# GNN layer with residual norm on one core: in the drain, GpSimd makes the selectors, the floor of the messages moves to PSUM, and TensorE turns the selectors between the two halves of the message sums

## What is computed

```python
def _L0_gnn_ref(x, edge_index, edge_attr, W, b, gamma, beta):
    row, col = (edge_index[0], edge_index[1])
    msg_in = jnp.concatenate([x[row], x[col], edge_attr], axis=-1)
    h = msg_in @ W + b
    mu = jnp.mean(h, axis=-1, keepdims=True)
    var = jnp.mean(jnp.square(h - mu), axis=-1, keepdims=True)
    h = (h - mu) * jax.lax.rsqrt(var + LN_EPS) * gamma + beta
    msg = jax.nn.relu(h)
    return jax.ops.segment_sum(msg, row, num_segments=x.shape[0])

x = _layernorm(x + _L0_gnn_ref(x, jnp.stack([src, dst]), edge_attr_128, W, b, gamma, beta), axis=-1)
```

## Time and profile before

| | before |
|---|---|
| median of 3 runs (lowest to highest) | 1763.23 us (1761.63 to 1763.72) |
| the profiled execution's own time | 1767.91 us |
| its span, first to last instruction | 1766.0 us |
| mean granted TensorE clock over the span | 0.813 |
| TensorE (PE) busy | 1214.0 us, 69% |
| DVE busy | 960.2 us, 54% |
| ScalarE (ACT) busy | 718.9 us, 41% |
| GpSimd (POOL) busy | 770.3 us, 44% |

### The profile page before, as it was taken

How to read it: one execution, slowest core, us unless ns; L and a number is a source line. 1 busy time by engine, 2 the same in 40 slices (tenths; PEclk the granted TensorE clock), 3 DMA queues, 4 the chain that set the end, 5 groups by cost and what they waited for, 6 DMA issues and landing times.

```text
span 1766.0 us, 36601 instructions
## 1 busy us (share of the span) xinstructions
PE 1214.0 (69%) x10009; PEld 1061.0 (60%) x10010; DVE 960.2 (54%) x2822; ACT 718.9 (41%) x2854; POOL 770.3 (44%) x808
## 2 busy tenths in 40 slices
PE   6688766676676766666666666766666766647775
PEld 5555656666566665666666566665656666546662
DVE  7633345555455555445545545554455545439997
ACT  4223333434334443334434434443334433336766
POOL 0334555444454445455444455444555444550003
PEclk9778788778778878788887888787788778869998
DMA  7544444444434444444444444444344434313322
GB/s 213 165 116 130 134 145 146 128 113 120 138 116 129 129 117 116 123 130 130 123 115 122 130 122 129 127 112 131 112 130 128 127 111 119 108 57 91 90 67 73
DMA packets 184266, 214.69 MB, mean 122 GB/s; under 512 B 51478, under 2 KB 133610, under 8 KB 184080
## 3 DMA queue, kind: packets, MB, share of 16 engines
q1 hardware_dynamic: 158044, 159.86, 33.8%
q0 software_dynamic: 25088, 51.83, 8.4%
q10 hardware_dynamic: 948, 0.79, 0.2%
HBM read 145.91 MB, written 66.47 MB: 120 GB/s over the span
## 4 chain that ended last, share of the span: by engine, by line
PE 41%; another core or an unknown queue 22%; issue 18%; ACT 9%; DVE 6%; DMA 2%; DVEq 2%; SPq 0%; ACTq 0%
PE bank L956 11%; PE bank L934 7%; PE bank L910 7%; PE bank L850 5%; ACT late L1177 4%; PE bank L924 3%; PE bank L963 2%; DVE late L1573 2%; ACT turn L1139 2%; PE bank L840 1%; PE bank L838 1%; DVEq L490 1%; DMA tabB<-room 1%; ACT late L1183 1%
## 5 line engine op out<-in xcount | busy, mean ns | idle before, releaser
L677 POOL DMA_INDIRECT rows<-p,pos_idx x784 | 754.3, 962 | 825.4 <-ACT p L1143 537.3
L1139 ACT COPY turn<-bank 128x512 f32<-128x512 f32 x196 | 114.8, 586 | 705.1 <-remote 533.1
L956 PE MATMUL bank<-wc,turn 128*128 128x128 f32 x1552 | 300.8, 354 | 67.4 <-ACT turn L1139 54.7
L934 PE MATMUL bank<-room 128*128 x2640 | 251.8, 250 | 93.7 <-issue 67.2
L956 PEld LDWEIGHTS bank<-wc,turn 128*128 128x128 f32 x1552 | 260.5, 254 | 92.2 <-ACT turn L1139 77.5
L934 PEld LDWEIGHTS bank<-room 128*128 128x128 bf16 x2640 | 208.7, 115 | 115.1 <-issue 104.0
L1177 ACT ACTIVATE late<-room 128x128 f32<-128x128 f32 x880 | 260.7, 302 | 3.0 <-issue 1.5
L1573 DVE SCALAR_TENSOR_TENSOR late<-room,late,floor 128x128 f32<-128x128 f32 x880 | 252.6, 349 | 0.8 <-issue 0.5
L910 PE MATMUL bank<-late 128*128 128x129 f32 x1504 | 233.3, 299 | 25.9 <-issue 23.5
L910 PEld LDWEIGHTS bank<-late 128*128 128x128 f32 x1504 | 211.8, 215 | 18.6 <-issue 18.2
L1169 ACT COPY room<-bank 128x512 bf16<-128x512 bf16 x220 | 129.2, 587 | 210.6 <-remote 111.1
(11 more groups left out here) (237 smaller groups left out, 1255.4 us busy)
## 6 DMA issues: line engine op xcount, KB each, us to landing
p<-in_edge_attr_dram SPq DMA_DIRECT2D x98, 512.0 KB
room<-rows SPq DMA_DIRECT2D x264, 129.0 KB
near_bc<-near SPq DMA_DIRECT2D x98, 256.0 KB
late<-rows SPq DMA_DIRECT2D x176, 129.0 KB
rows<-p,pos_idx POOLq DMA_INDIRECT x784
rows<-fill SPq DMA_DIRECT2D x49, 129.0 KB, 3.2
win<-tabB SPq DMA_DIRECT2D x196, 31.5 KB
tabB<-room SPq DMA_DIRECT2D x12, 384.0 KB, 3.2
```

Source lines behind the costliest of these rows:

```text
L677: nc.gpsimd.indirect_dma_start(rows_ap, bass.IndirectOffsetOnAxis(pos_idx[:, k, j:j + 1], 0), stage[:, k, j, :], None).then_inc(st_free[k] ...
L934: mm = pe.matmul(bank[A_BANK + b2][:, jj * D:(jj + 1) * D], selT[b2][:, jj * P:(jj + 1) * P], tabA[:, bass.ds(at[jj // UJ], 1), part, :], ...
L956: pe.matmul(bank[H_BANK + h][:, t * D:(t + 1) * D], eT[h][:, t * P:(t + 1) * P], wc[:, 2, :], start=(t == 0), stop=False, skip_group_check ...
L1139: nc.scalar.copy(eT[h], bank[E_BANK][:]).then_inc(eT_ready, 1)
```

## The change

Four edits, all in the drain. From step `BY_POOL` = 178 on, GpSimd makes the selectors (those of pair 180 and later), as 4 `tensor_scalar` instructions a step, one for each tile, in place of one DVE instruction; it waits for the loaded rows and for pair `s - 2` to be summed, as the DVE did. A copy of `floor` is put into PSUM (bank 3) by the DVE at step 177, and the messages of step 178 and later read that copy. In every drain step TensorE turns the selectors after the first two of the four tiles of the sum, and no longer ahead of the sum.

```diff
@@
+        floor_ps = bank[3][:, 0:D]
@@
+        BY_POOL = FUSED + 4
@@ gpsimd, behind the scatters
+            def selectors(s, c, q, r):
+                hk = hs_at(s, c, q, r, 2)
+                pool.wait_ge(hs_ready[hk[0]], hk[1] * 32)
+                pool.wait_ge(n_o, s - 1)
+                settle()
+                for j in range(SJ):
+                    a = nc.gpsimd.tensor_scalar(sel[(c + 2) % RING][:, j, :], iota_row[:], hs[hk[0]][:, j, D:ROW], None, ALU.is_equal)
+                a.then_inc(n_sel, 1)
+
+            def step(s, c, q, r, on):
+                if isinstance(s, int) and s < BY_POOL:
+                    return
+                if isinstance(s, int) and s == BY_POOL:
+                    pool.wait_ge(n_sel, BY_POOL + 2)
+                if on(2):
+                    selectors(s, c, q, r)
+            drain_trips(pool, trip_count(pool), step)
@@ tensor, drain step
                 if on(1):
                     at = entry(pe, regs, blk_i, s + 1, NB - 1)
-                    turn_selectors(s, c)
-                if on(-2):
-                    sum_pair(s, c)
+                for jj in range(SJ):
+                    if jj == SJ // 2 and on(1):
+                        turn_selectors(s, c)
+                    if on(-2):
+                        sum_tile(s, c, jj)
                 if on(1):
                     select_a(s, c, at)
@@ vector
-            def messages(s, c):
+            def messages(s, c, least=floor[:]):
@@
-                                                       floor[:], ALU.mult, ALU.max)
+                                                       least, ALU.mult, ALU.max)
@@ vector, drain step
                 if on(-1):
-                    messages(s, c)
-                if on(2):
+                    messages(s, c, floor[:] if isinstance(s, int) and s < BY_POOL else floor_ps)
+                if on(2) and isinstance(s, int) and s < BY_POOL:
                     selectors(s, c, q, r, iota_row[:])
+                if isinstance(s, int) and s == BY_POOL - 1:
+                    dve.wait_ge(st_ready, 2 * NG)
+                    nc.vector.tensor_copy(floor_ps, floor[:]).then_inc(s_floor_ps, 1)
+                    dve.wait_ge(s_floor_ps, 1)
```

More of the change, by code:

```diff
@@ L342, in bass_gnn_resnorm @@
         s_iota_ps = sem("iota_in_psum")
+        s_floor_ps = sem("floor_in_psum")
         s_rbase = sem("rank_bases_made")
```

## The result

| | before | after |
|---|---|---|
| median (lowest to highest) | 1763.16 us (1761.63 to 1763.72), 4 runs | 1792.46 us (1790.65 to 1794.01), 4 runs |
| ratio to before, 95% interval | | 1.0148 [1.0128, 1.0169] |
| the profiled execution's own time | 1767.91 us | 1790.65 us |
| its span | 1766.0 us | 1788.8 us |
| granted TensorE clock over the span | 0.813 | 0.826 |

The change makes the kernel 29.3 us slower; the forecast was 20.3. By the interval of the ratio it is between 22.6 and 29.8 us.

A forecast was written before the change was run, and what follows sets the result against it. The drain was taken as bound by the DVE (11.51 us a loop turn), TensorE's instruction stream 1% behind (11.4). Terms: 21.6 less 1.3, less 0.5, plus 0.5: +20.3 us, median 1783.5; range 1775 to 1794, chance 0.79.

The forecast's parts named there:

- The turn between the halves: TensorE's drain step: half a sum leaves part of the copy uncovered; +0.54 us a step, 21.6 over 40 steps.
- four parts of the new path: TensorE, sum to select: half sum 0.45, turn to copy 0.53, copy 0.59, release 0.15; 1.72 us against 1.18.
- The relief of the DVE: Selectors off the DVE in the drain: its step falls from 2.88 to 2.28 us; gain of 1.3 us.
- Floor in PSUM: Drain messages reading the floor from PSUM: between -0.06 and +0.06 us for each of four, taken as zero.
- The price by the Trainium skill's rule: DVE instructions with two SBUF inputs and GpSimd's SBUF reads block each other; the price if floor stayed in SBUF.
- Selectors on GpSimd: Drain selectors at 0.35 us an instruction, 1.4 a step, start 0.9 behind the turn; cost zero, deciding only from 0.57.
- rival (b): GpSimd binds the drain: at 0.75 us an instruction or with exclusion, step 4.0 us, 1811 us; chance 0.08.
- (b)'s milder case: Mere exclusion between messages and GpSimd's selectors at 0.35 us each: step 3.45 us, 6 us more, 1790.
- It scatters nothing in the drain.: GpSimd's queue in the drain: no scatters there, so no DMA stands behind it.
- (a): TensorE's sequencer runs ahead in the drain, hiding the register load's 0.78 us: step 2.59 us, 1752 us; chance 0.07.
- (c): Clock falls to 0.50 in the drain as TensorE's busy share drops: step about 3.8 us, 1804 us; chance 0.02.
- (d): Change hardly does anything: copy covered by both halves, only the 1.3 us relief remains, 1762 us; chance 0.04.

The follow-up runs named there:

- before_read_ahead: Kernel before with only TensorE's register load for the next step moved behind the sum, ahead of the select: 1253.65 us, ratio 1.0005.
- turn_only: Kernel before with only the turn put between the halves of the sum; selectors on the DVE, floor in SBUF: 1272.8 us against 1253.49, ratio 1.0149.
- turn_read_ahead: Kernel turn_only with TensorE's register load for the next step moved behind the sum, ahead of the select: 1251.83 us against 1253.32, ratio 0.9987.
- floor_sbuf: The change with the floor of the messages read from SBUF throughout: 1282.31 us, ratio 1.0231 to the kernel before.
- pool_half: The change with two of four selectors on GpSimd and two on the DVE, from row numbers in PSUM: 1275.56 us, ratio 1.0172 to before.
- pool_cols64: The change with each GpSimd selector instruction cut to 64 of 128 columns: 1275.75 us in one run, 22.4 above before.
- half_read_ahead_2: Kernel before with register load read ahead, two of four selectors on GpSimd from step 178, floor and row numbers in PSUM: 1247.17 us, ratio 0.9973.
- half_later_2: Kernel of half_read_ahead_2 with GpSimd's two selectors from step 180 on instead of 178: 1244.73 us, ratio 0.9944 to before.
- pool_old_order: The change with the turn back ahead of the whole sum; selectors on GpSimd, floor in PSUM: 1310.55 us, ratio 1.044 to before.

## Why the prediction was right, and where it was off

**What bounds the kernel before.** The reading held that the DVE binds and TensorE's stream is a close second. Taking TensorE's load out of the path leaves before's time unchanged (before_read_ahead), and the 0.23 us between selectors and turn were not a wait, since a real one is 0.05. (The DVE's step is nine instructions, 362 in 40 steps, and not seven as the prediction counts; nothing rests on it.)

**The turn between the halves, +20.3 us with the relief.** This mechanism was right. turn_only measured +19.3, with each of the four parts of the new path within 0.01 us of its forecast. From select to next sum it takes 1.58 us, 1.57 was foretold. before_read_ahead and turn_read_ahead show that the order is dear only together with the register load: with the load out of the path the same order costs nothing that can be measured.

**The relief of the DVE, at most 1.3 us.** The prediction subtracts 1.3 us for it, but with TensorE's step at 3.29 no relief of a DVE at 2.88 can count. The 1.3 us are the distance from TensorE's own step in before to the DVE's, which the lengthening uses up first. turn_only shows it: it has no relief, and costs no more than forecast with it. The sum came out the same, and only the name of the term was wrong.

**Floor in PSUM, zero.** A message takes 342 ns against 346, and the messages end no step: right. The price by the Trainium skill's rule ("SBUF — State Buffer", "Who interferes with whom") was not paid in floor_sbuf; but as hardly a message ran beside GpSimd there, no run here shows it either way.

**Selectors on GpSimd, cost zero: the term that was mis-sized.** The prediction took 0.35 us an instruction, near the value scaled from the `tensor_tensor`, with 0.962 as the far bound. It measured 0.603 (a pitch of 0.58), just above the 0.57 from which the same paragraph said that GpSimd decides. Its start behind the turn was put at 0.9 us and measured 1.10: the second half's loads take 0.53 and not 0.45, and its last matmul and the signal the rest. Together 1.10 + 2.34 + 0.05 = 3.49 against TensorE's 3.29. That is rival (b), to which the prediction gave a chance of 0.08, with the very sign it named for it, turns that follow GpSimd's end by 0.05 us. Its price, 0.2 us a step, is that of (b)'s milder case, but that case had exclusion as its cause, and here it is the length of the instructions. It is paid in three of four steps, and makes 26.2 instead of 19.8 us over the last 40 steps (20.3 less the 0.5 for the first steps): **6.4 us**. pool_half and pool_cols64 take it away in two ways and return to 3.29. The scaling went wrong mostly in the fixed part: 0.1 us of start and 0.28 of streaming were assumed, and the two lengths measured give some 0.28 and 0.32.

**"It scatters nothing in the drain."** True of the trace it was read from. On the chips with the clock near 0.95 it is false, and costs once: 2.4 us between half_read_ahead_2 and half_later_2.

**Rivals.** (a) did not happen: select to sum took 1.58 us and nothing of it was hidden. Done by hand, by reading the registers ahead, it gives back what the prediction said it would, up to the DVE's bound. (c) did not happen in the change (granted clock 1.00; TensorE was 74% busy in the drain, where the prediction had 66), and happened in pool_old_order, where TensorE waits 1.9 us a step in one piece. (d) is excluded by turn_only.

**The total.** 1783.5 forecast, 1792.46 measured, inside the range of 1775 to 1794 and near its end. It is inside partly by luck: the range worked out for the forecast's own mechanism ended at 1790, and the last 4 us had been added for GpSimd, though for another cause on it. Of the 9 us between, 6 are GpSimd's. The other 3 are not located. The drain's own loss is 26.2 to 26.5 us in the profile, and 26.3 was the difference of medians the second time, inside the interval of the first, so I take them for the spread between comparisons.

## What to carry to other kernels

Where two engines are within a per cent of being the bound, relieving one brings next to nothing, and lengthening the other's path costs nearly in full; look at the sequencer's loads and branches before calling an engine idle. Do not split the work that covers a copy unless something else covers it: here half a sum of 0.53 us could not hide a copy that takes 1.26 from turn to select. Before moving work to another engine, measure one instruction of it, and look at what stands ahead of it in that engine's queue on a chip where the other stages run faster.

## What the runs showed that I had not expected

- GpSimd's `tensor_scalar` with a per-partition operand takes 0.603 us for 128 columns in f32 and 0.441 for 64; four `scalar_tensor_tensor` of the same size on the DVE take 1.12 us, GpSimd's four compares 2.34.
- The same kernel takes 1763 us on one chip and 1253 on another, at a mean granted clock of 0.81 and near 0.95. The ratio of the clocks is 1.17 and that of the times 1.41, so the clock alone does not account for it; the cause was not sought. In the loop of the drain, at 1.00 on both, steps agree to 0.01 us.
- With a wait of 1.6 to 1.9 us in every step (pool_old_order) the granted clock went back and forth between its levels, a mean of 0.77 over 40 us; with two shorter waits in a step, of some 0.5 and 0.7 us (the change, turn_only), it stayed at 1.00 in the loop. That the one led to the other is not shown.
